# A permutation matrix in 16 bits, widened on another engine, and a new order of tasks

## The chip, the cores and the metric

One core of a Trainium2 chip. The metric is the device time of one execution in microseconds (us), the median of several runs.

## What is computed

32 graphs of 256 nodes: `x` is 32 x 256 x 64, `adj` 32 x 256 x 256 and sparse (about 1.5% of the pairs, and the diagonal). For each graph:

```python
mask = (adj > 0.0)
xj_proj = x @ W1[:F]
diff = x[:, :, None, :] - x[:, None, :, :]
h = relu(xj_proj[:, :, None, :] + diff @ W1[F:] + b1)      # H = 192
hm = einsum('bjkh,bjk->bjh', h, mask)
out = layernorm(x + hm @ W2 + sum(mask, -1)[..., None] * b2)
```

So each node j adds up relu(u_j - v_k) over its neighbours k, with u = x (W1a + W1b) + b1 and v = x W1b.

## The kernel before, in words

**Tiling.** Two graphs make a pair, 16 pairs in all. A pair has TILES = 4 tiles of P = 128 nodes. The 192 hidden columns are split into a "main" part (128, one group per tile) and a "tail" part (64, the two graphs packed together).

**A pair's path.** VectorE makes the 0/1 mask from the adjacency tiles (`masks`, L1583), counts neighbours (`count_masks`, `count_least`, `count_rest`) and compares the counts with levels (`sort_key`). TensorE adds that up (`keys`), and VectorE turns it into a rank for each node (`ranks`) and into a permutation matrix that sorts nodes by their number of neighbours (`permutation`, L1650): 1 where the place equals the rank. TensorE transposes and permutes the masks with it (`turn_masks`), ScalarE copies them out of PSUM (`copy_maskT`), TensorE numbers each node's neighbours (`number_slots`), ScalarE copies that (`copy_slots`), and VectorE makes one-hot matrices, one for each "slot", the j-th neighbour of every node (`select`, pieces 0 to 10). TensorE sorts x (`sort_x`, with the permutation in f32, `excess_tail` beside it), forms u (`hidden_u_main`, `hidden_u_tail`) and v (`hidden_v`); ScalarE copies u, and v in two forms (`high_v` f16, `full_v` f32), and GpSimd (POOL) takes the difference (`low_v`, L661). ScalarE writes u into PSUM banks (`seed`), TensorE adds the gathered neighbours' -v (`gather`, L1327), and VectorE adds relu of the result into `sums` (`add`, L1796; the last units are shared, `add_joint`, L1810). At the end come `project`, `copy_y`, `unsort_y` (with the transposed permutation from `turn_perm` and `copy_permT`), `add_residual`, `statistics`, and on POOL `moments`, `centre` and `scale`.

**The permutation's type.** `perm` is f32, because `sort_x` multiplies f32 by it. The matmuls in 16 bits read it through `perm16()`, the upper half of each f32 word:

```python
def perm16(side, c):
    return perm[side][:, c, :].bitcast(BF16).rearrange("p (r two) -> p r two", two=2)[:, :, 1]
```

**Scales.** Because v is split into f16 parts, the weights are scaled by a power of two. For pair 0 that comes from the maximum of its x (`first_max`) and of the weights (`prepare_weights`, L1675, on VectorE; `add_weights_up`, L1120, on TensorE; `weight_top`, L1680, and `first_scales`, L1695 to L1712, on VectorE), for all others from all of x: ScalarE sums it in four chunks (`sum_chunk`, L815), VectorE takes the most (`most`), TensorE spreads it (`spread_x`, L1132), and VectorE makes the scales (`scales`). `hidden_u_main(Pair(0, 0))` and `hidden_u_tail(Pair(0, 0))` wait for `scales_ready[0]`. `keep_busy` (L1375) and `set_banks` (L1143) are matmuls on ones.

**What sets the order.** Every engine has its own list of tasks, in program order, with semaphores between them. Each list has a head that is written out (pairs 0 and 1), a `body(pair)` run for pairs 1 to 13 (of these, 4 to 9 in a hardware loop of two pairs a turn), and a written-out tail (pairs 14 and 15). In one body, different engines work on up to five different pairs. A task waits at its place in the list, and with it all that stands behind it on that engine. The buffers of most tiles are double, by the pair's parity. SyncE issues all DMAs through one queue, in its own list: first `adj` 0, constants, x 0, weights, xT 0, `adj` 1, all of x in four chunks, x 1, xT 1, `adj` 2, `adj` 3, then x 2, which waits for `xb_ready` (from `residual(Pair(0, 0))` on POOL) and `xs_ready`.

In the head VectorE runs, in this order: `masks` to `sort_key` of pair 0, `ranks`, `permutation`, `ranks_above`, `prepare_weights`, `masks(Pair(0, 1))`, `count_masks(Pair(0, 1))`, `count_given(Pair(0, 0))`, `count_least(Pair(0, 1))`, `first_max`, `weight_top`, `first_scales`, `masks(Pair(0, 2))`, then selections of pair 0, `most` and `scales`.

Should a graph have more neighbours than the slots hold, a general path runs behind all this (`general_loop`); with these inputs it doesn't.

## Time and profile before

| what | value |
|---|---|
| runs, device time | 252.63, 252.81, 254.0 us; median 252.81 |
| profiled execution | 252.74 us, span 250.9 us |
| busy | PE 235.9 (94%), VectorE 226.6 (90%), ScalarE 209.8 (84%), POOL 121.4 (48%) |
| DMA | 18.20 MB, the 16 engines at 21.7% of the span |

The span runs from the first to the last instruction that the profile shows, and the device time has some 2 us around it. Names: PE is TensorE's matmul, PEld its weight load, DVE VectorE, ACT ScalarE, POOL GpSimd, SP SyncE. L1327 is a line of the kernel. Matmuls are pipelined and their spans overlap. An instruction on VectorE or ScalarE starts some 0.1 us before the one ahead of it ends, so the time from start to start is a little shorter than the duration.

### The profile page before, as it was taken

What the parts mean: (1) busy time and instruction counts of PE and PEld (TensorE: products, weight loads), DVE (VectorE), ACT (ScalarE), POOL (GpSimd) and SP (SyncE); (2) the same over time, 40 slices, a digit from 0 to 9 for tenths busy, and PEclk for the clock granted to TensorE, in tenths of its full rate; (3) what the DMA queues carried; (4) which work ended last, traced back from release to release, by engine and by line L of the source; (5) the groups of instructions that cost most, each with busy time, mean ns of one, the idle gap of its engine ahead of it and who ended that gap; (6) DMA issues with size and microseconds to landing.
All of it is one profiled execution on the core that took longest, in us unless ns stands there. A gap on an engine that the chain in (4) does not pass through costs nothing. (4 is left out here: it accounts for less than half of the span.)

```text
span 250.9 us, 9244 instructions
## 1 busy us (share of the span) xinstructions
PE 235.9 (94%) x2810; PEld 188.7 (75%) x2813; DVE 226.6 (90%) x778; ACT 209.8 (84%) x572; POOL 121.4 (48%) x288
## 2 busy tenths in 40 slices
PE   7947989999999999999999999999999999998992
PEld 2524758888787878787888878887878888886761
DVE  4757699999999999999999999999999999997763
ACT  2384888989998989899899999898999989987631
POOL 1124444363645637463736364563736483576225
PEclk9985899999999999999999999999999999999998
DMA  6983003221212213131313021221310110000002
GB/s 201 357 325 106 3 4 123 70 84 30 70 54 78 73 55 96 44 107 42 106 39 107 14 74 59 64 82 47 105 44 25 43 46 0 25 24 1 3 8 63
DMA packets 10550, 18.20 MB, mean 73 GB/s; under 512 B 1296, under 2 KB 7696, under 8 KB 10512
## 3 DMA queue, kind: packets, MB, share of 16 engines
q1 hardware_dynamic: 10512, 17.73, 21.7%
q8 instruction: 19, 0.31, 0.5%
q14 instruction: 19, 0.16, 0.2%
HBM read 15.63 MB, written 2.10 MB: 71 GB/s over the span
## 5 line engine op out<-in xcount | busy, mean ns | idle before, releaser
L1327 PE MATMUL ring<-hot,vh 128*128 128x128 bf16 (+9 forms) x768 | 117.4, 255 | 1.3 <-ACT ring L914 1.0
L1327 PE MATMUL ring<-hot,vl 128*128 128x128 bf16 (+9 forms) x768 | 116.3, 251 | 0.0
L1796 DVE SCALAR_TENSOR_TENSOR sums<-ring,sums 128x256 f32<-128x256 f32 (+10 forms) x240 | 97.8, 428 | 4.3 <-PE ring L1327 1.9
L1327 PEld LDWEIGHTS ring<-hot,vh 128*128 128x128 f16 (+1 forms) x768 | 62.0, 104 | 23.6 <-issue 16.8
L1327 PEld LDWEIGHTS ring<-hot,vl 128*128 128x128 f16 (+1 forms) x768 | 61.9, 103 | 2.4
L661 POOL TENSOR_TENSOR vl<-vf,vh 128x384 f16<-128x384 f32 x32 | 29.7, 929 | 63.2 <-ACT vf L870 59.4
L903 ACT COPY ring<-u_sb 128x192 f32<-128x192 f32 (+8 forms) x160 | 49.3, 359 | 7.4 <-DVE sums L1796 7.4
L900 ACT COPY ring<-u_sb 128x512 f32<-128x512 f32 (+1 forms) x80 | 43.3, 559 | 0.4 <-issue 0.2
L715 POOL TENSOR_TENSOR sums<-taken,sums 128x512 f32<-128x512 f32 x16 | 20.7, 1292 | 27.1 <-ACT taken L932 27.1
L821 ACT CAST maskT<-bx 128x512 bf16<-128x512 f32 x32 | 18.5, 586 | 14.3 <-PE bx L1171 13.8
L1771 DVE TENSOR_SCALAR hot<-slotT 128x944 bf16<-128x944 f16 (+6 forms) x112 | 28.6, 280 | 0.0
L1591 DVE TENSOR_REDUCE counts<-mask 128x8 f32<-128x1024 bf16 x16 | 19.4, 1214 | 0.1
L828 ACT CAST slotT<-bx 128x512 f16<-128x512 f32 x32 | 18.9, 592 | 0.0
L1290 PEld LDWEIGHTS bx<-w2ms,sums 128*128 128x128 f32 x128 | 17.9, 192 | 1.3 <-DVE sums L1824 0.6
L1304 PE MATMUL bx<-y_sb,permT 128*128 128x64 f32 x128 | 18.6, 272 | 0.0
L1290 PE MATMUL bx<-w2ms,sums 128*128 128x64 f32 x128 | 17.9, 263 | 0.4 <-DVE sums L1824 0.4
L863 ACT CAST vh<-bx 128x384 f16<-128x384 f32 x32 | 15.4, 482 | 3.2 <-PE bx L1257 3.2
L1304 PEld LDWEIGHTS bx<-y_sb,permT 128*128 128x128 f32 x128 | 16.6, 191 | 0.9 <-ACT y_sb L884 0.5
L1188 PE MATMUL bx<-maskT,cst_half 128*128 128x128 bf16 x128 | 16.1, 221 | 0.1
L1583 DVE TENSOR_SCALAR mask<-adj_sb 128x1024 bf16<-128x1024 f32 x16 | 11.0, 688 | 5.4 <-DMA adj_sb<-adj 5.4
L1257 PE MATMUL bx<-w1vs,xT_sb 64*128 64x192 f32 x128 | 15.5, 362 | 0.3 <-ACT u_sb L855 0.3
L870 ACT COPY vf<-bx 128x384 f32<-128x384 f32 x32 | 15.5, 489 | 0.0
(119 smaller groups left out, 463.7 us busy)
## 6 DMA issues: line engine op xcount, KB each, us to landing
adj_sb<-adj SPq DMA_DIRECT2D x16, 512.0 KB, 3.7
x_sb<-x_pairs SPq DMA_DIRECT2D x16, 128.0 KB, 2.3
xT_sb<-xT SPq DMA_DIRECT2D x16, 128.0 KB, 2.1
x_all<-x SPq DMA_DIRECT2D x4, 512.0 KB, 7.9
out<-o_sb SPq DMA_DIRECT2D x16, 128.0 KB, 1.7
wts<-weights SPq DMA_DIRECT2D x1, 417.0 KB, 4.8
cst_general<-general SPq DMA_DIRECT2D x1, 256.0 KB, 3.2
cst_half<-half SPq DMA_DIRECT2D x1, 137.0 KB, 3.1
```

The lines of the kernel that those rows point to most:

```text
L661: eng.tensor_tensor(vl[pair.side][:, c, :], vf[:, c, :], vh[pair.side][:, c, :], ALU.subtract).then_inc(vl_ready, 1)
L715: eng.tensor_tensor(to, taken[piece][:, :, :], to, ALU.add).then_inc(taken_added, 1)
L821: eng.copy(maskT[:, g * NT:g * NT + NT, :].rearrange("p t r -> p (t r)"), (bx1, bx2)[g][:, :]).then_inc(maskT_copied, 1)
L828: eng.copy(slotT[:, g * NT:g * NT + NT, :].rearrange("p t r -> p (t r)"), (bx0, bx1)[g][:, :]).then_inc(slots_copied, 1)
L900: last = eng.copy(to, u.unsqueeze(1).broadcast_to([P, sum(map(whole, pieces)), n, P]))
L903: last = eng.copy(view(pair, part, unit, piece), u[:, :, 0:PIECES[piece][2]])
L1290: eng.matmul(to[:, g * O:g * O + O], sums[pair.side][:, NT + g * NT + t, :], w2ms[scaled(pair)][:, :], start=(g == 0), stop=False, skip_gr ...
L1304: last = eng.matmul(bx3[:, (TILES + c) * O:(TILES + c + 1) * O], permT[pair.side][:, c, :], y_sb[:, t * 2 + g, :], start=True, stop=True)
L1327: return eng.matmul(to if part == "main" else to[g * HT:g * HT + HT], values, selection, start=False, stop=final, skip_group_check=True)
L1591: eng.tensor_reduce(counts[pair.side][:, :, :].rearrange("p g c -> p (g c)"), mask[pair.side][:, :, :].rearrange("p c (k n) -> p (c k) n", ...
L1771: eng.tensor_scalar(to[:, :, :, off:off + n], slots, float(MARK + s), None, ALU.is_equal).then_inc(hot_ready, 1)
L1796: eng.scalar_tensor_tensor(out=to, in0=view(pair, part, unit, piece), scalar=0.0, in1=to, op0=ALU.max, op1=ALU.add).then_inc(added[part], 1)
```

## The change

`permutation` writes a bf16 tile `perm16` (`rank` becomes f16), and a new ScalarE task copies it to the f32 tile `perm`, for `sort_x` alone. The bf16 matmuls read `perm16` densely. The lists of all engines but SyncE are put in another order, most of all in head and tail.

```diff
-        rank = sb("rank", [P, TILES])
-        perm = both("perm", [P, TILES, P])
+        rank = sb("rank", [P, TILES], F16)
+        perm16, perm = both("perm16", [P, TILES, P], BF16), both("perm", [P, TILES, P])
...
+            def widen_perm(pair):
+                eng.wait_ge(perm_ready, pair.n + 1)
+                if pair.follows(2):
+                    eng.wait_ge(xs_ready, pair.n - 1)
+                eng.copy(perm[pair.side][:, :, :].rearrange("p c r -> p (c r)"),
+                         perm16[pair.side][:, :, :].rearrange("p c r -> p (c r)")).then_inc(perm_widened, 1)
...
-                                          perm16(pair.side, g * NT + t), start=True, stop=True)
+                                          perm16[pair.side][:, g * NT + t, :], start=True, stop=True)
...
             def sort_x(pair):
-                eng.wait_ge(perm_ready, pair.n + 1)
+                eng.wait_ge(perm_widened, pair.n + 1)
...
-                eng.tensor_tensor(perm[pair.side][:, :, :], places.unsqueeze(1).broadcast_to([P, TILES, P]),
+                eng.tensor_tensor(perm16[pair.side][:, :, :], places.unsqueeze(1).broadcast_to([P, TILES, P]),
                                   rank[:, :].unsqueeze(2).broadcast_to([P, TILES, P]), ALU.is_equal).then_inc(perm_ready, 1)
```

The loop bodies. ScalarE: `widen_perm(new)` ahead of `copy_maskT(new, 0)`, and `copy_permT` goes from the end of the body to the start of the next. VectorE: `add(older, "tail", 7)` goes behind `select(old, 9)`. POOL: `scale(older)` goes between `low_v(new, 0)` and `low_v(new, 1)`. TensorE: `gather(new, "main", 6)` is no longer cut in two across the loop's edge.

VectorE's head:

```diff
             sort_key(Pair(0, 0))
+            first_max()
             ranks(Pair(0, 0))
             permutation(Pair(0, 0))
             ranks_above(Pair(0, 0))
+            count_given(Pair(0, 0))
+            masks(Pair(0, 1))
+            masks(Pair(0, 2))
             prepare_weights()
-            masks(Pair(0, 1))
-            count_masks(Pair(0, 1))
-            count_given(Pair(0, 0))
-            count_least(Pair(0, 1))
-            first_max()
             weight_top()
             first_scales()
-            masks(Pair(0, 2))
+            make_ident()
+            count_masks(Pair(0, 1))
             select(Pair(0, 0), 0)
             select(Pair(0, 0), 1)
             select(Pair(0, 0), 2)
-            most()
             select(Pair(0, 0), 3)
             select(Pair(0, 0), 4)
+            count_least(Pair(0, 1))
+            most()
+            select(Pair(0, 0), 5)
+            count_rest(Pair(0, 1))
             scales()
-            count_rest(Pair(0, 1))
-            select(Pair(0, 0), 5)
             scale_down(0)
-            make_ident()
             run(eng, body)
```

TensorE's head:

```diff
             turn_masks(Pair(0, 0), 1)
+            add_first_up()
+            number_slots(Pair(0, 0), 0)
+            number_slots(Pair(0, 0), 1)
             add_weights_up()
-            number_slots(Pair(0, 0), 0)
             sort_x(Pair(0, 0))
+            excess_tail(Pair(0, 0))
             keep_busy(1)
-            number_slots(Pair(0, 0), 1)
-            excess_tail(Pair(0, 0))
-            add_first_up()
             keep_busy(3)
+            hidden_u_tail(Pair(0, 0))
+            hidden_u_main(Pair(0, 0))
             set_banks(0)
-            excess_main(Pair(0, 0))
-            hidden_u_main(Pair(0, 0))
-            hidden_u_tail(Pair(0, 0))
             spread_x()
             hidden_v(Pair(0, 0))
+            keys(Pair(0, 1))
+            excess_main(Pair(0, 0))
             set_banks(1)
-            keys(Pair(0, 1))
...
```

ScalarE's head becomes: `widen_perm(0)`, the two `copy_maskT`, `sum_chunk(0)`, `copy_slots(0)`, `sum_chunk(1)`, `copy_xs`, `copy_slots(1)`, `sum_chunk(2)`, `copy_u_tail`, `sum_chunk(3)`, `copy_u_main`, `full_v(0)`, `high_v(0)`, a seed, `high_v(1)`, `full_v(1)`, `widen_perm(1)`, all for pair 0 but the last. POOL's head becomes: `degrees`, `corrections`, `add_weights`, `degrees(1)`, `low_v(0, 0)`, `corrections(1)`, `low_v(0, 1)`, `scale_inputs`, `add_taken(0)`, `low_v(1, 0)`, `degree_bias(0)`, `degrees(2)`, `scale_outputs(1)`, `residual(0)`, `scale_outputs(0)`, `low_v(1, 1)`, `corrections(2)`, `degree_bias(1)`.

In the tail the lists of pairs 14 and 15 are interleaved anew. At its end TensorE runs `unsort_y(14)`, `project(15)`, `unsort_y(15)`, `keep_busy_last(2)`, `add_over` (before: `add_over` ahead of `project(15)`, `keep_busy_last(2)` ahead of `unsort_y(15)`), and ScalarE's `sum_over` stands behind `deviation(14)`; POOL's `scale(14)` waits for that sum in both.

## Rows read from the trace of the kernel before

**Rows 1.** Busy time by stretch (stretch, its length, each engine, granted clock, DMA share).

```profile
7.00:17.23 10.23, 8.03 (x62) 4.34 (x61) 6.04 (x18) 6.98 (x15) 2.33 (x5) 1.00 1.00 380
17.23:27.47 10.24, 6.96 (x45) 4.71 (x47) 8.21 (x30) 5.42 (x13) 4.94 (x11) 0.50 0.24 82
...
40.53:206.00 165.47, 165.31 (x2122) 138.00 (x2117) 163.50 (x565) 153.92 (x426) 86.20 (x204) 1.00 0.22 68
...
123.43:137.24 13.81, 13.81 (x185) 11.66 (x183) 13.74 (x48) 12.84 (x36) 6.84 (x16) 1.00 0.28 94
```

**Rows 2.** What VectorE waited for, 40.53 to 205 (total us, times, longest).

```profile
DVE sums L1796 <- PE ring L1327: 0.3, 1, 0.3
```

**Rows 3.** Groups by line and form (busy us, mean ns), VectorE.

```profile
L1650 DVE TENSOR_TENSOR perm<-cst_half,rank 128x512 f32<-128x512 f16 x16 | 11.0, 686 | 0.0
...
L1776 DVE TENSOR_TENSOR hot<-slotT,cst_half 128x288 bf16<-128x288 f16 x16 | 7.4, 464 | 0.0
...
L1762 DVE TENSOR_TENSOR hot<-slotT,cst_half 128x512 bf16<-128x512 f16 x16 | 6.7, 420 | 0.0
...
L1627 DVE TENSOR_TENSOR reaches<-rest,cst_order 128x72 bf16<-128x72 bf16 x16 | 3.6, 228 | 0.1
```

**Rows 4.** The same view, ScalarE.

```profile
L900 ACT COPY ring<-u_sb 128x512 f32<-128x512 f32 x64 | 37.2, 603 | 0.2 <-issue 0.2
...
L815 ACT ACTIVATE x_abs<-x_all 128x1024 f32<-128x1024 f32 x4 | 4.2, 1062 | 0.9 <-DMA x_all<-x 0.9
```

**Rows 5.** SyncE's issue of `adj_sb` 2 and 3; issues 8.4 to 10; x loads.

```profile
8.54 2.15 SPq L514 DMA_DIRECT2D adj_sb<-adj  x2
...
adj_sb<-adj SPq DMA_DIRECT2D x1, 512.0 KB, 8.6
...
x_sb<-x_pairs SPq DMA_DIRECT2D x16, 128.0 KB, 2.3
```

**Rows 6.** Order of time (start us, us), VectorE, 0 to 42.

```profile
8.83 0.34 DVE L1675 SCALAR_TENSOR_TENSOR w_abs<-wts 64x192 f32<-64x192 f32 x1
...
12.04 0.35 DVE L1680 TENSOR_REDUCE w_top<-ring 128x1 f32<-128x192 f32 x1
12.77 0.22 DVE L1695 TENSOR_SCALAR bound<-ring,w_top 128x1 f32<-128x1 f32 x1 [0.39 <-PE ring L1125]
...
13.53 0.88 DVE L1711 TENSOR_SCALAR w1abs<-w1ab,up_bits 128x256 f32<-128x256 f32 x1
...
17.20 0.69 DVE L1583 TENSOR_SCALAR mask<-adj_sb 128x1024 bf16<-128x1024 f32 x1 [2.55 <-DMA adj_sb<-adj]
...
22.52 0.22 DVE L1636 TENSOR_TENSOR steps_ahead<-bx,reaches 128x64 f32<-128x64 f32 x1 [0.88 <-PE bx L1155]
...
29.53 0.50 DVE L1759 TENSOR_SCALAR hot<-slotT 128x512 bf16<-128x512 f16 x2 [1.62 <-ACT slotT L828]
```

**Rows 7.** The same view, TensorE.

```profile
9.39 0.59 PE L1120 MATMUL ring<-w_abs,ones 64*128 64x192 f32 x2
...
10.55 0.66 PE L1201 MATMUL bx<-perm,x_sb 128*64 128x128 f32 x8
...
14.47 0.70 PE L1236 MATMUL bx<-xs,w1abs 64*128 64x256 f32 x4 [0.41 <-DVE w1abs L1711]
...
18.75 0.80 PE L1132 MATMUL ring<-ident,x_most 128*128 128x128 f32 x2 [2.15 <-DVE x_most L1685]
19.48 1.65 PE L1257 MATMUL bx<-w1vs,xT_sb 64*128 64x192 f32 x8
21.06 1.03 PE L1143 MATMUL ring<-ones 128*128 128x512 bf16 x2
...
40.53 0.61 PE L1201 MATMUL bx<-perm,x_sb 128*64 128x128 f32 x8
```

**Rows 8.** What ScalarE waited for, 40.53 to 206.

```profile
ACT maskT L821 <- PE bx L1171: 4.9, 17, 0.8
```

**Rows 9.** What VectorE waited for, 40.53 to 250.9.

```profile
DVE sums L1810 <- ACT small L939: 2.2, 3, 1.6
```

More of the change, by code:

```diff
@@ L740, in body @@
                     low_v(new, 0)
[L741 removed]
                 if has(-2):
                     scale(older)
+                if has(1):
+                    low_v(new, 1)
                 if has(2):
@@ L959, in body @@
                 elder, older, old, new = pair.at(-3), pair.at(-2), pair.at(-1), pair.at(1)
+                if has(-1):
+                    copy_permT(old)
                 if has(0):
@@ L1002, in body @@
                     seed_joint(old)
-                if has(0):
-                    copy_permT(pair)
             eng.wait_ge(consts_loaded["single"], 16)
+            widen_perm(Pair(0, 0))
             copy_maskT(Pair(0, 0), 0)
@@ L1642, in ranks @@
                         eng.wait_ge(above_ready, pair.n)
-                eng.tensor_reduce(rank[:, :], steps_ahead[:, :, :], AX.X, ALU.add).then_inc(ranks_ready, 1)
+                with nc.allow_low_precision(reason="whole numbers of at most 128"):
+                    eng.tensor_reduce(rank[:, :], steps_ahead[:, :, :], AX.X, ALU.add).then_inc(ranks_ready, 1)
             def permutation(pair):
@@ L1899, in body @@
                     select(old, 9)
+                if has(-2):
+                    add(older, "tail", 7)
                 if has(0):
```

222 lines of the change are left out of this document (110 added, 112 removed).

## The prediction

> **What bounds the kernel now.** I read four views in this order: the busy time by stretch, what VectorE waited for, the groups by line and form, and the order of time of the head. In one period of the middle (the loop works one pair in 13.81 us) VectorE is busy for 13.74 us, and over 40.53 to 206.00 for 163.50 of 165.47 us [rows 1]. In that whole stretch its waits come to 0.3 us [rows 2]. TensorE shows 100% busy too, but its matmul spans overlap, so that share alone proves nothing; that VectorE never waits does. So VectorE sets the middle: only VectorE time that is removed shortens a pair, and a task that is only moved there changes nothing while its inputs are in time. ScalarE is busy for 12.84 us of the period and has 0.97 us free [rows 1]. The head, up to about 29.5 us, is another matter: there each engine waits, and what counts is the chain that ends in the first selections of pair 1. Whatever the head is late, the middle is late by, since nothing in the middle is idle to catch up.
>
> The time: the span is 250.9 us and the profiled execution took 252.74, 1.8 us more around the span; the median of the runs is 252.81. I add to the median.
>
> **The permutation in 16 bits.** It is 128x512 on VectorE, one per pair, at 686 ns [rows 3]. Its result becomes bf16, `rank` becomes f16 and `places` is f16 already. What decides is how fast such an instruction runs when one input is a single value repeated along the innermost dimension (`rank` broadcast over 128). Three rows with 16-bit tensors on both sides bear on it [rows 3]. L1762, 512 elements, both inputs with neighbouring elements, takes 420 ns. L1776 is 288 elements, its `slotT` operand repeated along the innermost dimension, and takes 464 ns: more than the 512 of L1762. L1627, 72 elements with `rest` repeated in the same way, takes 228 ns. From L1627 to L1776 there are 216 elements and 236 ns, 1.09 ns each; carried on to 512 that gives 464 + 224 x 1.09 = 708 ns, and the full-width row is 686. The new instruction is built like L1776 and L1627, so I take 686 ns still: **0 us saved**. The other end is L1762's 420 ns, 0.266 us for each of 16 pairs, 4.3 us. The two small instructions on `rank` have 64 elements and can save nothing that counts.
>
> The Trainium skill weighs on both sides here. "VectorE: DVE Perf Modes", perf-mode tier table, gives `tensor_tensor` on bf16 in SBUF twice the rate: the sum would then be 4.3 us lower, the first rival. "Vector Engine (DVE) Microarchitecture Reference", section 5.1, wants a step of plus or minus 1 on every operand and reports one element read again and again in a two-source operation at the 1x rate; by that rule nothing is saved, and L1776 agrees with its 464 ns.
>
> **The widening** is new on ScalarE: 128x512 bf16 to f32, SBUF to SBUF, 16 times. The nearest row is L900, 512 elements from SBUF at 603 ns; the far end is L815, 1024 elements at 1062 ns [rows 4]. I take 0.6 us, some 0.52 from start to start. A period's ScalarE work goes from 12.84 to 13.4 us, under 13.81. Its place is just ahead of the two mask copies, where ScalarE waits for TensorE anyway: 4.9 us in 17 waits over the middle, about 0.3 at each [rows 8]. The two waits of a pair hide the 0.52 us; the first mask copy ends about 0.3 us later, and the slot numbering behind it on TensorE comes half a microsecond after that copy. So I cost it at **0 in the middle**. If that cover were gone it would be 0.5 us a pair. `sort_x` now waits for the widening, but comes a whole pair later. TensorE's reading of every second 16-bit word goes; I give it 0, since VectorE is the bound.
>
> **The moves in the loop.** On VectorE the tail addition of piece 7 goes behind two selections; all inputs are early, 0. On POOL `scale` goes between the two `low_v`, on ScalarE `copy_permT` merely crosses the loop's edge, on TensorE the last gather is no longer cut: 0, none of these engines is the bound.
>
> **The head: this is where the time goes.** VectorE runs its list in order, and `masks(Pair(0, 2))` now stands ahead of `prepare_weights`, `weight_top` and `first_scales`. Its adjacency tiles are issued at 8.54 us and land 8.6 us later, 17.2 us, in a stretch in which the DMA engines are 100% busy [rows 1, 5]; SyncE's list is not touched, so that landing stays. Before, the third mask waited for it too, for 2.55 us, but with the scales of pair 0 already done; `w_abs` ran at 8.83 and `w1abs` ended at 13.53 + 0.88 = 14.41 [rows 6].
> Step by step, at the half TensorE clock of 17.23 to 27.47 (0.50 granted, that is 1.2 GHz; it fell after a stretch with TensorE partly idle, and the new order leaves it idler, so I keep the fall) [rows 1]:
> - masks 17.20 to 17.81, `w_abs` 0.34: 18.15.
> - `add_weights_up` on TensorE, 0.59 us at full clock, about 0.9 at half: 19.2. TensorE stands at it from about 11.5 us, and behind it wait `sort_x(0)`, so the copy of xs on ScalarE, and behind that two of the four sums over x.
> - `w_top` 0.35, then from `bound` to the end of `w1abs` as before, 14.41 - 12.77 = 1.64: 21.2.
> - TensorE meanwhile: `sort_x`, 0.66 at full clock, some 0.9 here; the excess, its four small matmuls, some 0.3; four busy matmuls at about half of the 1.03 that the two of `set_banks` took at this clock, less their overlap: 21.8. Then `hidden_u_tail` and `hidden_u_main`, 0.70 at full clock for the second, about 1.0 each here: 23.8. `set_banks(0)`, 1.03 with its overlap: 24.7. VectorE has `most()` done by 24.5, after the counts, five selections and the fourth sum over x.
> - `spread_x` 0.8, and `hidden_v(0)` 1.65 at this clock: it starts at 25.5 and ends at 27.1. Before it started at 19.48 [rows 7]: **6.0 us late**.
> - From there the old chain: v copied, keys, ranks of pair 1 at about 28.3 instead of 22.52, 5.8 late. The first selection of pair 1 had 1.6 us of waiting before it at 29.53 [rows 6], of which the new order keeps about 0.7: **4.9 us late** at 34.4. There the period begins, and the lag stays.
> Ends: 4.0 us, if TensorE is back at full clock early and the selections wait less; 6.0 if nothing is recovered.
> Also moved on POOL: `residual(Pair(0, 0))` now stands behind `low_v` of pair 1, at some 36 us, and SyncE's load of x for pair 2 waits for it with four loads queued behind. Done at about 42.5, with the 4.9 in it, and 2.3 us to land [rows 5], it is there by 45; pair 2 was sorted at 40.53 [rows 7], 45.4 with the 4.9. So 0, but the cover is thin: each tenth more on POOL would hold TensorE by a tenth, once.
>
> **The tail.** VectorE waits there for ScalarE's clamps, 2.2 us in three waits, and for little else [rows 9]. A new order can recover at most those and about 1.5 us of others; nothing excludes a loss, for `sum_over` now ends only after the last `unsort_y`, with `scale(14)` behind it on POOL. I take -0.8, ends -2.6 and +0.7.
>
> **Sum:** 0 + 0 + 4.9 - 0.8 = +4.1; 252.8 + 4.1 = 256.9, which I put as **256.8 us**, 1.6% slower. Its own range is 254.5 to 258.9.
>
> **Rivals.**
> 1. The permutation runs at L1762's rate, 420 ns. Then VectorE, the bound, loses 16 x 0.266 = 4.3 us and pays for the head: 256.8 - 4.3 = 252.5, no change that can be measured (I count 0.5% as that, 1.3 us). It decides from about 0.2 us saved a pair. For: all its tensors have 16 bits. Against: L1776 and L1627. 0.14; a third of it with a better tail is faster.
> 2. The masks' wait is off the path: the tiles of pair 2 land early, or the scales are not the last thing `hidden_v` needs. The head is then the old one, the tail gives 0.8 to 1.3: 251.5, faster. It decides from a landing before about 12 us. Against: DMA at 100% and an untouched SyncE list. 0.06.
> 3. ScalarE becomes the bound. If the widening costs nearer L815's 1062 ns, the second mask copy is 0.4 us later in each pair, and its few waits for VectorE's additions no longer fit: about 0.3 us x 14 = 4.2 us, 261.0. For: 13.4 of 13.81 us. Against: the waits it falls into. 0.08.
> 4. TensorE's clock stays at 1.2 GHz for one more stretch, since it idles from 11.5 to 18.2. The first gathers would run at half rate: about 4 us more, 260.8. Against: from 17.2 to 27.5 it does about as much as before, after which the clock came back [rows 1]. 0.10.
>
> **How the numbers follow.** Forecast 0.62; rivals 0.14, 0.06, 0.08, 0.10. Slower: 0.62 + 0.08 + 0.10 = 0.80. Same: most of rival 1, 0.10. Faster: rival 2 and the rest of rival 1, 0.10. The range takes in rival 1's 252.5 and the nearer half of rivals 3 and 4: 252.3 to 260.5. Both signs do not share the weight, so it is the forecast's range widened.
>
> **What would show it.** In the new profile: the third mask on VectorE still at 17.2, with an idle time of nearly 7 us before it; `w1abs` of pair 0 ending at about 21 instead of 14.4; `hidden_v(0)` at about 25.5; the permutation at 686 ns; a period of 13.81 us; ScalarE 13.4 us busy in it. The forecast falls if the permutation row shows 420 ns, if the period is not 13.8 us, or if `hidden_v(0)` starts before 22 us.

## The result and the profile after

| | kernel before | changed kernel |
|---|---|---|
| median of the runs | 253.03 us (252.63 to 254.0, 4 runs) | 261.17 us (260.89 to 261.94, 4 runs) |
| profiled execution, span | 252.74, 250.9 us | 261.94, 260.1 us |
| VectorE, ScalarE busy | 226.6, 209.8 us | 227.7, 216.9 us |

The ratio of the times is 1.0321 [1.0283, 1.0358]: 3.2% slower, 8.1 us, where 256.8 was forecast (252.3 to 260.5). The same kernel run again beside other runs of the kernel before (15) gave 260.31 us against 252.98, 1.0269 [1.0232, 1.0306]; so the loss is 7 to 8 us. One of those six runs, 262.86 us, is in the slow state, and all ratios are of fast runs alone. The two profiled executions differ by 9.2 us, and that is the sum which the rows below divide.

The busy time by stretch, to set beside [rows 1] (the first two stretches end where the granted clock changes in this kernel):

```profile
7.00:12.30 5.30, 3.32 (x31) 2.01 (x31) 2.82 (x7) 2.28 (x4) 1.03 (x3) 1.00 0.99 340
12.30:22.50 10.20, 4.01 (x19) 2.46 (x20) 3.71 (x12) 3.68 (x9) 0.00 (x0) 0.50 0.52 203
40.53:206.00 165.47, 163.52 (x2078) 135.52 (x2077) 162.96 (x561) 158.01 (x435) 88.03 (x204) 1.00 0.23 71
123.43:137.24 13.81, 13.78 (x177) 11.44 (x175) 13.74 (x48) 13.29 (x38) 7.30 (x18) 1.00 0.21 65
```

A window of 13.81 us in the middle has VectorE busy for 13.74 us, as before; ScalarE went from 12.84 to 13.29. The period itself is 13.6 us in both kernels: the 11 pairs from pair 2's first sums to pair 13's take 149.63 us before and 149.68 after. The loss is not in the middle. The groups by line, ScalarE's widening and mask copy, then the permutation on VectorE:

```profile
L818 ACT CAST perm<-perm 128x512 f32<-128x512 bf16 x16 | 10.0, 623 | 7.1 <-DVE perm L1658 7.1
L825 ACT CAST maskT<-bx 128x512 bf16<-128x512 f32 x32 | 18.1, 589 | 1.3 <-PE bx L1180 1.1
```
```profile
L1658 DVE TENSOR_TENSOR perm<-cst_half,rank 128x512 bf16<-128x512 f16 x16 | 10.9, 682 | 0.0
```

The permutation still takes 682 ns (686 in f32, [rows 3]). From 40.53 to 206 the mask copy waits for TensorE for 0.3 us, where it was 4.9 [rows 8]: the widening has eaten those waits. Without it, under the same new orders (2), they are 5.1 us.

VectorE in order of time (start us, us), beside [rows 6]:

```profile
17.48 0.69 DVE L1590 TENSOR_SCALAR mask<-adj_sb 128x1024 bf16<-128x1024 f32 x1 [6.78 <-DMA adj_sb<-adj]
18.09 0.34 DVE L1683 SCALAR_TENSOR_TENSOR w_abs<-wts 64x192 f32<-64x192 f32 x1
19.53 0.36 DVE L1688 TENSOR_REDUCE w_top<-ring 128x1 f32<-128x192 f32 x1 [1.09 <-PE ring L1129]
...
20.76 0.35 DVE L1719 TENSOR_SCALAR w1abs<-w1ab,up_bits 128x256 f32<-128x256 f32 x1
...
27.81 0.23 DVE L1643 TENSOR_TENSOR steps_ahead<-bx,reaches 128x64 f32<-128x64 f32 x1 [0.71 <-PE bx L1164]
...
34.05 0.49 DVE L1767 TENSOR_SCALAR hot<-slotT 128x512 bf16<-128x512 f16 x2 [0.64 <-ACT slotT L832]
```

And TensorE, beside [rows 7]:

```profile
18.49 1.00 PE L1129 MATMUL ring<-w_abs,ones 64*128 64x192 f32 x2 [7.58 <-DVE w_abs L1683]
...
25.64 0.92 PE L1266 MATMUL bx<-w1vs,xT_sb 64*128 64x192 f32 x8 [0.25 <-ACT u_sb L849]
...
46.10 0.66 PE L1210 MATMUL bx<-perm,x_sb 128*64 128x128 f32 x8 [0.89 <-DMA x_sb<-x_pairs]
```

This is the chain that was forecast: VectorE waits 6.78 us at the third mask with the weights behind it, TensorE then 7.58 us for `w_abs`, and `hidden_v(0)` starts at 25.64 instead of 19.48. The last of these rows is the loss that was not forecast there: the sort of pair 2's x waits for its load.

The tail, all engines in order of time:

```profile
251.18 1.94 PE L1313 MATMUL bx<-y_sb,permT 128*128 128x64 f32 x8 [0.46 <-ACT y_sb L888]
...
253.90 0.37 PE L1371 MATMUL bx<-over,ones 128*1 128x64 f32 x2
...
254.31 0.21 ACT L959 ACTIVATE over_junk<-bx 1x64 f32<-1x64 f32 x1 [2.99 <-PE bx L1371]
...
254.68 0.46 POOL L720 CAST over_int<-over_sum 1x1 int32<-1x1 f32 x1 [2.51 <-ACT over_junk L959]
255.10 0.60 POOL L675 TENSOR_TENSOR o_sb<-centred,rstd 128x256 f32<-128x256 f32 x1
...
255.81 0.18 DVE L1856 RECIPROCAL rstd<-std 128x4 f32<-128x4 f32 x1 [0.71 <-POOL o_sb L675]
```

The last `rstd` is held by POOL's `scale(14)`, that by the sum of `over`, and that by `add_over`, which TensorE runs behind the last `unsort_y` and two scratch matmuls.

The 9.2 us, each as the difference of the same instruction's start in the two traces, and beside it the same steps in the profiled execution of 15, the same kernel once more (rounded, so the columns can be 0.1 off their sums). "First sums" is `start_sums`, L1750 here and L1742 before.

| step, us later than in the kernel before | changed | changed again (15) |
|---|---|---|
| head, to the first sums of pair 1 (41.25 against 36.72; the first selection, 34.05 against 29.53, says the same) | 4.5 | 5.6 |
| load of x for pair 2, to the first sums of pair 13 (206.03 against 200.29) | 1.2 | 1.1 |
| interleaving, to `z` of pair 14 (248.54 against 242.30) | 0.5 | 0.5 |
| last `unsort_y`, 1.94 us at the half clock, to `z` of pair 15 (253.16 against 246.08) | 0.8 | 0.0 |
| the sum's chain, to VectorE's last instruction (256.08 against 248.20) | 0.8 | 0.1 |
| behind it, mostly the last store | 1.3 | 1.2 |
| span | 9.2 | 8.5 |

### The profile page after: what moved, and what is told of

Read it like the earlier page. It is cut to its first block, busy times and chain, and to the rows that moved or that the text cites. A ratio compares the mean times of both kernels' runs of the same rounds, so it can differ in the third digit from the quotient of the medians.

```text
span 260.1 us, 9280 instructions
## 1 busy us (share of the span) xinstructions
PE 235.8 (91%) x2813; PEld 187.6 (72%) x2813; DVE 227.7 (88%) x778; ACT 216.9 (83%) x588; POOL 122.7 (47%) x288
## 4 chain that ended last, share of the span: by engine, by line
PE 64%; DVE 8%; issue 8%; POOL 5%; ACT 5%; DMA 5%; SPq 3%; DVEq 0%; POOLq 0%; ACTq 0%
PE ring L1336 31%; PE bx L1266 4%; PE bx L1313 4%; PE bx L1299 4%; DMA adj_sb<-adj 3%; PE bx L1245 3%; PE bx L1302 3%; PE bx L1210 3%; PE bx L1253 2%; PE bx L1180 2%; DVE sums L1804 2%; PE bx L1197 2%; DVE sums L1750 2%; PE bx L1234 1%; DMA x_sb<-x_pairs 1%
## 5 line engine op out<-in xcount | busy, mean ns | idle before, releaser
L907 ACT COPY ring<-u_sb 128x192 f32<-128x192 f32 (+8 forms) x160 | 49.9, 359 | 7.2 <-DVE sums L1804 6.8
L1313 PE MATMUL bx<-y_sb,permT 128*128 128x64 f32 x128 | 19.4, 281 | 0.5 <-ACT y_sb L888 0.5
L1313 PEld LDWEIGHTS bx<-y_sb,permT 128*128 128x128 f32 x128 | 17.4, 200 | 1.0 <-ACT y_sb L888 0.7
L611 POOL TENSOR_TENSOR excess<-deg,given 128x4 bf16<-128x4 f32 x16 | 4.1, 256 | 25.5 <-DVE given L1675 25.5
L818 ACT CAST perm<-perm 128x512 f32<-128x512 bf16 x16 | 10.0, 623 | 7.1 <-DVE perm L1658 7.1
```

Source lines behind the costliest of these rows:

```text
L907: last = eng.copy(view(pair, part, unit, piece), u[:, :, 0:PIECES[piece][2]])
L1313: last = eng.matmul(bx3[:, (TILES + c) * O:(TILES + c + 1) * O], permT[pair.side][:, c, :], y_sb[:, t * 2 + g, :], start=True, stop=True)
```

## The experiments

The first four are about the types, the next six about the head, the rest about the tail. Ratios are to the kernel before, run on the same chip; its medians lay between 252.91 and 253.08.

### 1. The types alone

The kernel before with the new tiles and the widening (and the wait of `sort_x` for it), all orders old.

```diff
+                    widen_perm(new)
                     copy_maskT(new, 0)
```

> The kernel before with the types alone: bf16 perm16 by VectorE, widened by ScalarE ahead of the two mask copies, every list in its old order. Theory (VectorE sets the middle and takes 686 ns either way; the widening falls into ScalarE's waits): 253.0 us, within 0.5, period 13.6 us on average. Rival A (16 bits help, 420 ns): 249. Rival B (ScalarE becomes the bound): over 255.

Measured: 253.51 us, 1.0021 [1.0001, 1.0041]. The groups by line, and the middle window:

```profile
L1659 DVE TENSOR_TENSOR perm<-cst_half,rank 128x512 bf16<-128x512 f16 x16 | 11.0, 686 | 0.0
```
```profile
123.43:137.24 13.81, 13.81 (x187) 11.64 (x184) 13.74 (x48) 13.22 (x37) 6.87 (x16) 1.00 0.26 86
```

The 16 bits save nothing and the widening costs nothing per pair; 0.2% is all that both do to the kernel.

### 2. The orders alone

The changed kernel with the permutation in f32 and no widening.

```diff
-                    widen_perm(new)
                     copy_maskT(new, 0)
```

> The changed kernel with all new orders, but the permutation in f32 as before and no widening on ScalarE. Theory (VectorE takes 686 ns for it either way and ScalarE's 0.6 us falls into its waits): same period of 13.6 us on average, median 261.2 within 0.4. Rival A (the widening costs in the middle): 0.1 us or more a pair, 259.6 or less. Rival B (reading every second 16-bit word slows TensorE): slower than 261.6.

Measured: 262.34 us, 1.0366 [1.0339, 1.0394]. From pair 4's first sums to pair 13's, 84.42 to 206.76, it is 122.34 us; with the widening 83.73 to 206.03, 122.30. Taking the widening off ScalarE gives nothing back: rival 3 falls. With 1, the whole loss is in the orders. The time is 1 to 2 us above the changed kernel's, past the 261.6 us from which the expectation counted for its rival B. But the matmuls of `turn_masks`, which read the permutation, take 219 ns with every second word (L1172 here) and 219 ns densely (L1180), so that rival isn't borne out; where the extra microsecond comes from is open.

### 3. VectorE's prices by themselves

Seven scratch instructions in the wait for the third mask of the changed kernel. `every` is the places repeated over the 4 tiles, `again` the rank repeated along the row, `other` a plain row repeated over the tiles.

```diff
+            eng.tensor_tensor(m16[0][:, :, :], every, other, ALU.is_equal)
+            eng.tensor_tensor(m32[0][:, :, :], every, other, ALU.is_equal)
+            eng.tensor_tensor(m16[1][:, :, :], every, again, ALU.is_equal)
+            eng.tensor_tensor(m16[2][:, :, :], again, every, ALU.is_equal)
+            eng.tensor_tensor(m32[1][:, :, :], every, again, ALU.is_equal)
+            eng.tensor_scalar(m16[3][:, 0, :], places, rank[:, 0:1], None, ALU.is_equal)
+            eng.tensor_scalar(m16[4][:, 0, :], places, 3.0, None, ALU.is_equal)
```

> The changed kernel with seven extra instructions on VectorE that write scratch tiles nobody reads, in the 6.8 us in which VectorE waits for the tiles of the third mask. It measures VectorE's prices by themselves: the places repeated over the three tiles compared with a tile's rank repeated along the row (384 elements), written in 16 bits, with the operands swapped, and written in 32 bits; the same with a plain 128-element row as second operand, written in 16 and in 32 bits; and one 128-element comparison with a scalar read from a tile and one with a constant. Theory that the repeated rank (an operand whose innermost step is zero) is what keeps the permutation at 686 ns: the three forms with the rank repeated take 650 to 700 ns whatever the output and the order, the 16-bit form without it takes 400 to 480 ns. Rival, that the 16-bit output never helps where the operands are repeated over the tiles: the form without the rank takes about 680 ns too. For the scalar form the run of four scalars gave 270 ns; if the scalar from a tile is the reason, the constant takes about 190 ns. All seven together are some 3.5 us and lie in the wait, so the time stays at 260 to 262 us.

Measured: 261.77 us. The groups by form, VectorE, 8 to 20 us (the lines L1974 to L1980 are the seven, in that order):

```profile
L1975 DVE TENSOR_TENSOR m<-cst_half 128x512 f32<-128x512 f16 x1 | 0.7, 679 | 0.0
L1977 DVE TENSOR_TENSOR m<-rank,cst_half 128x512 bf16<-128x512 f16 x1 | 0.7, 679 | 0.0
L1976 DVE TENSOR_TENSOR m<-cst_half,rank 128x512 bf16<-128x512 f16 x1 | 0.7, 678 | 0.0
L1978 DVE TENSOR_TENSOR m<-cst_half,rank 128x512 f32<-128x512 f16 x1 | 0.7, 677 | 0.0
L1974 DVE TENSOR_TENSOR m<-cst_half 128x512 bf16<-128x512 f16 x1 | 0.4, 410 | 0.0
...
L1979 DVE TENSOR_SCALAR m<-cst_half,rank 128x128 bf16<-128x128 f16 x1 | 0.2, 242 | 0.0
...
L1980 DVE TENSOR_SCALAR m<-cst_half 128x128 bf16<-128x128 f16 x1 | 0.2, 180 | 0.0
```

Both conditions are needed: a 16-bit result and no operand repeated along the innermost dimension give 410 ns; either one missing gives 677 to 679, and the order of the operands changes nothing. (The operands have 4 x 128 = 512 elements; the expectation's 384 was a slip, its times were for these instructions.) Repeating over the tiles does no harm.

### 4. Four scalars in place of the repeated rank

The types of 1, and the permutation as four instructions that read the rank as a scalar per partition.

```diff
+                for c in range(TILES):
+                    last = eng.tensor_scalar(perm16[pair.side][:, c, :], places, rank[:, c:c + 1], None, ALU.is_equal)
```

> As the kernel with the types alone, but the permutation is made by four TENSOR_SCALAR instructions of 128 elements, each with one column of rank (f32) as its per-partition scalar, so that no operand repeats one element. Theory: each takes about 190 ns, 0.10 to 0.15 us from start to start as the 128-element selection does, 0.4 to 0.55 us in all against 0.61 for the one of 686 ns; VectorE as the bound passes that on: 0.05 to 0.2 us a pair, 250 to 252.3 us. Rival (reading the scalar costs as much as is saved, or VectorE is not the bound): 252.8 to 253.5.

Measured: 255.45 us, 1.0098 [1.0069, 1.0128], above the expected range and above the rival's too. The group, and two of its pairs in order of time:

```profile
L1660 DVE TENSOR_SCALAR perm<-cst_half,rank 128x128 bf16<-128x128 f16 x64 | 13.1, 270 | 0.0
```
```profile
36.84 0.74 DVE L1660 TENSOR_SCALAR perm<-cst_half,rank 128x128 bf16<-128x128 f16 x4
...
50.83 1.40 DVE L1660 TENSOR_SCALAR perm<-cst_half,rank 128x128 bf16<-128x128 f16 x4
```

The mean of 270 ns hides two sorts. 62 of the 64 take 242 to 255 ns and start 0.16 us apart, so that four of them hold VectorE for 0.65 us up to the start of the next instruction, where the one instruction held it for 0.60. In two pairs, at 23.15 and 50.83 us, one of the four takes 0.91 us, both times while a `low_v` of POOL is running. Pair 13's first sums are 2.07 us late: 1.4 from these two, the rest from 0.05 us in each other pair. A scalar read from a tile costs 242 to 255 ns where a constant costs 180 (3), so this way round the repeated rank is no saving.

### 5. The third mask behind the head

The changed kernel, one task moved.

```diff
             masks(Pair(0, 1))
-            masks(Pair(0, 2))
             prepare_weights()
...
             scale_down(0)
+            masks(Pair(0, 2))
             run(eng, body)
```

> The changed kernel with one line moved: the third mask of VectorE's head goes from ahead of prepare_weights to behind scale_down(0). Theory (the wait for the adjacency tiles of pair 2 holds the whole head, 4.5 us): w_abs at about 10.7 us instead of 18.1, hidden_v(0) at 18 to 19 instead of 25.64, the median falls by 4 to 5.5 us from 261.2, to 255.7 to 257.2. Rival (the head is late for other reasons, the new lists of TensorE and ScalarE): hidden_v(0) stays behind 23 us and the median above 259.

Measured: 253.17 us, 1.0025 [0.9981, 1.0069]: 7 to 8 us back from one line, more than expected. VectorE and TensorE in order of time:

```profile
10.74 0.34 DVE L1683 SCALAR_TENSOR_TENSOR w_abs<-wts 64x192 f32<-64x192 f32 x1
...
19.33 0.68 DVE L1590 TENSOR_SCALAR mask<-adj_sb 128x1024 bf16<-128x1024 f32 x1
```
```profile
18.40 0.92 PE L1266 MATMUL bx<-w1vs,xT_sb 64*128 64x192 f32 x8 [0.25 <-ACT u_sb L849]
```

`hidden_v(0)` starts 7.2 us earlier than in the changed kernel and 1.1 earlier than in the kernel before. The wait for pair 2's x is gone here, with `residual(0)` at its new place. In another profiled execution of the same kernel (span 253.6 us instead of 251.4) `hidden_v(0)` starts at 18.42 and pair 13's first sums at 199.46, 6.6 us earlier than in the changed kernel, but there the wait is back:

```profile
39.61 0.66 PE L1210 MATMUL bx<-perm,x_sb 128*64 128x128 f32 x8 [0.41 <-DMA x_sb<-x_pairs]
```

So the late head is not the only thing that decides on that wait (see 10). Pair 13's first sums are also 0.8 us ahead of the kernel before, and that is no gain of the other moves: with the old orders and the third mask last (8) they come at 198.73, earlier still. The expectation had priced the mask's wait in the changed kernel and left out what this mask costs at its old place, 1.5 us (8).

### 6. The third mask back where it was

The changed kernel with the mask behind `first_scales`.

```diff
-            masks(Pair(0, 2))
             prepare_weights()
             weight_top()
             first_scales()
+            masks(Pair(0, 2))
             make_ident()
```

> The changed kernel with the third mask moved only behind first_scales, the place that it had relative to weight_top and first_scales in the kernel before; the rest as changed. Theory, that what costs is VectorE waiting for the tiles with the weights queued behind it: w_abs starts at about 10.5 us, hidden_v(0) at 18.5 to 20 instead of 25.64, and the time is 253.2 to 255, 1 at most above the version with the mask behind scale_down(0). Rival, that at this place the mask still waits (its tiles landed at about 17.2, first_scales ends at about 13 here because ident is made behind it): VectorE waits some 3 to 4 us with the selections of pair 0 behind it, hidden_v(0) is at 19 to 21, start_sums of pair 1 at 38 to 39.5, and the time is 255 to 257.5.

Measured: 257.7 us, 1.0203 [1.0161, 1.0245]; the rival's case, a little past its upper end. VectorE:

```profile
13.22 0.35 DVE L1719 TENSOR_SCALAR w1abs<-w1ab,up_bits 128x256 f32<-128x256 f32 x1
...
17.12 0.69 DVE L1590 TENSOR_SCALAR mask<-adj_sb 128x1024 bf16<-128x1024 f32 x1 [3.32 <-DMA adj_sb<-adj]
```

The scales are early, but the tasks which the change has moved behind this point (`count_least`, `most` and the selections) now wait 3.32 us, and `hidden_v(0)` starts at 20.98. What counts is which work stands behind the wait: with all of it behind, 261; with half, 257.7; with none, 253.2.

### 7. The masks' move alone, on the kernel before

```diff
+            masks(Pair(0, 1))
+            masks(Pair(0, 2))
             prepare_weights()
-            masks(Pair(0, 1))
             count_masks(Pair(0, 1))
...
             first_scales()
-            masks(Pair(0, 2))
```

> One part of the change alone on the kernel before: masks(1) and masks(2) moved ahead of prepare_weights, permutation, tail and the other orders left as they were. Theory, that this move is the head's whole loss: VectorE waits for the tiles of the third pair until about 17.2 us as in the changed kernel, hidden_v(0) starts at about 25.6 instead of 19.48, start_sums of pair 0 and 1 come 4.5 to 5.5 us later, and the time is 257 to 260, 1.6 to 2.8 per cent over. Rival, that the other reorderings of the head (the orders of the ranks and of the weights' part on TensorE and ScalarE) carry half of it: 254.5 to 256.

Measured: 260.4 us, 1.0269 [1.0229, 1.0309]. The mask is at 17.29 behind 6.58 us of waiting, and TensorE:

```profile
27.75 0.92 PE L1257 MATMUL bx<-w1vs,xT_sb 64*128 64x192 f32 x8 [1.33 <-ACT u_sb L845]
```

That one move alone costs 7.3 us, a little more than the expected range. Pair 13's first sums are 8.6 us late (208.84), more than the 5.7 of the full change: TensorE's list here keeps the slot numbering behind `add_weights_up`, so more stands in the wait, and the granted clock is at 0.5 for one more stretch (30.8 to 37.6).

### 8. The mask last, on the kernel before

```diff
             first_scales()
-            masks(Pair(0, 2))
...
             make_ident()
+            masks(Pair(0, 2))
             run(eng, body)
```

> The kernel before with its third mask moved from behind residual(0) to behind make_ident, so that VectorE's w_abs, w_top and w1abs and TensorE's w_bound come without it. Theory, that the mask ahead of the weights delays the head in either kernel: here VectorE does not wait for its tiles, so only the mask's own time ahead of w_abs goes and hidden_v(0) starts at 17.9 to 19.5 instead of 19.48; the time is 251 to 252.5, 0.2 to 0.8 per cent under the kernel before. Rival, that the head of the kernel before is set by the ranks and by the clock: no difference, 252.5 to 253.5.

Measured: 251.59 us, 0.9945 [0.9923, 0.9967], the only version under both kernels. The mask runs at 19.26 without any wait and `hidden_v(0)` starts at 18.30. The 2.55 us that the kernel before waits at its third mask [rows 6] were worth 1.5 us.

### 9. The clock during the wait

The changed kernel, TensorE's idle wait filled.

```diff
             number_slots(Pair(0, 0), 1)
+            keep_busy(28)
             add_weights_up()
```

> The changed kernel with 28 more scratch matmuls on TensorE in the 7.6 us that it idles ahead of add_weights_up; nothing else moves. It separates the wait from the clock: if part of what the third mask cost at the head is TensorE's granted clock falling in or behind its idle wait (0.5 from 12.3 to 22.5 us in the changed kernel, 17.2 to 27.5 in the kernel before), the stretches at 0.5 move and the time falls by 1 to 3 us, to 258 to 260. Theory that the wait alone costs: the stretches may move, but start_sums of pair 0 and 1 stay within 0.3 us and the time stays at 260 to 261.5. Rival on the other side: the scratch matmuls bring the half clock over hidden_v and the ranks, and the time rises by 1 to 4 us, to 261.5 to 265.

Measured: 260.28 us, 1.0272 [1.0243, 1.0301]. The busy time by stretch, to be read against the stretches above:

```profile
12.30:22.50 10.20, 9.08 (x50) 3.98 (x47) 4.31 (x14) 4.64 (x11) 0.45 (x1) 1.00 0.51 200
...
27.70:31.20 3.50, 2.98 (x30) 2.60 (x29) 2.44 (x6) 2.96 (x7) 2.41 (x6) 0.51 0.01 2
```

With the wait filled the granted clock stays at 1.00 (2.4 GHz) from 12.3 to 22.5 us, where it was 0.50 (1.2 GHz) with TensorE busy for 4.01 of 10.20 us. `hidden_v(0)` comes at 23.92 instead of 25.64, pair 1's first sums at 40.34 instead of 41.25, and the profiled execution took 259.39. Another 1.0 us of its gain is not the clock: the load of x for pair 2 landed 2.0 us after its issue and TensorE did not wait for it. The median does not follow: 260.28 against 261.17 and 260.31 for the changed kernel on other chips. The half clock is part of the head's loss in the traces, but what it is worth in the median, between nothing and 1 us, stays open.

### 10. The residual early

The changed kernel.

```diff
             add_weights()
+            degree_bias(Pair(0, 0))
+            residual(Pair(0, 0))
             degrees(Pair(0, 1))
...
             low_v(Pair(0, 1), 0)
-            degree_bias(Pair(0, 0))
             degrees(Pair(0, 2))
             scale_outputs(1)
-            residual(Pair(0, 0))
```

> The changed kernel with degree_bias(0) and residual(0) on POOL put back behind add_weights, so that the load of x for pair 2 is issued at once. Theory (the 0.89 us that TensorE waits for this load at 45 us is passed on in full by the middle, where nothing is idle): that wait goes, the start of sums of pair 2 stands 1.0 to 1.2 us earlier, median 260.0. Rival (VectorE catches it up, as it has waits around it): same median, 261.2.

Measured: 260.99 us, 1.0305 [1.0275, 1.0335]. The sort of pair 2's x starts with no wait, and pair 2's first sums come 14.0 us after pair 1's instead of 15.1. The wait is gone as expected, but the time is nearer to the rival's 261.2 than to the theory's 260.0 and cannot be told from the changed kernel's. In a profiled execution the half clock lasts from 12.1 to 25.7 us and puts pair 1's first sums at 42.43 instead of 41.25. Besides, the wait isn't always there to be saved: with `residual(0)` at its new place, the load landed 3.4, 3.3 and 3.4 us after its issue in the profiled executions of the changed kernel, of 15 and of 2, and 2.0 us after it in those of 3, 9 and 11, where pair 2's first sums come 14.1 us after pair 1's as well. The 1.2 us is shown in some of the traces, not in the medians.

### 11. The sum early

The changed kernel, with `sum_beyond` behind `add_taken(Pair(0, 15), 0)` on POOL as well.

```diff
             unsort_y(Pair(0, 14))
+            add_over()
             project(Pair(0, 15))
             unsort_y(Pair(0, 15))
             keep_busy_last(2)
-            add_over()
...
             clamp_small(Pair(0, 15))
+            sum_over()
             copy_y(Pair(0, 15))
             deviation(Pair(0, 14))
-            sum_over()
```

> The changed kernel with the sum over what is left beyond the slots taken early again: sum_beyond behind add_taken(15) on POOL, add_over ahead of project(15) on TensorE, sum_over ahead of copy_y(15) on ScalarE. Theory (all engines' branch waits for this sum; scale(14) on POOL stands behind it, and TensorE's branch, 3.7 us long, is exposed when it starts only at 256.0): rstd of pair 15 0.7 us earlier after z, TensorE's branch ends before the last store has landed, median lower by 1.5 to 2.1 us, 259.1 to 259.7. Rival (the last store is the end anyway): at most 0.7 us lower, 260.5.

Measured: 259.3 us, 1.0241 [1.0214, 1.0269]. The last `rstd` comes 1.52 us after the one before it instead of 2.31 and no longer waits for POOL. In 15, where the last `unsort_y` of the changed kernel ran at full clock, the distance was 1.62 us with the sum still late: 0.1 us of the 0.8 is the order, the rest comes with the half clock. Behind VectorE's last instruction the span goes on for 3.4 us instead of 4.1 (3.9 in 15). Against the changed kernel's 260.31 and 261.17 the median is 1 to 2 us lower, as expected.

### 12. The sum late, on the kernel before

The same tasks moved the other way; TensorE's part is shown, and on ScalarE `sum_over` goes behind `deviation(14)`, on POOL `keep_sum` behind `centre(14)`.

```diff
             unsort_y(Pair(0, 14))
-            add_over()
             project(Pair(0, 15))
-            keep_busy_last(2)
             unsort_y(Pair(0, 15))
+            keep_busy_last(2)
+            add_over()
```

> The kernel before with the order of the sum's parts alone taken from the changed kernel: add_over behind the last unsort_y and the scratch matmuls on TensorE, sum_over behind the last copy_y and deviation(14) on ScalarE, keep_sum behind centre(14) on POOL. Theory, that the late sum holds the last pair's scale and then the kernel's end through TensorE's branch: the last rstd comes about 2.3 us behind the one before it instead of 1.5, the branch of 3.6 us begins behind the last store instead of 2.4 us ahead of it, and the time rises by 1.3 to 2.2 us, to 254.3 to 255.3 (ratio 1.005 to 1.009). Rival, that the sum is late only because the interleaving before it is: no difference, 252.6 to 253.6.

Measured: 253.92 us, 1.0049 [1.0029, 1.0070], just short of the expected rise. Only 0.15 us of it is at the last `rstd` (248.09 against 247.94); the rest is behind it. The trace's records of branches, which the views by engine leave out, have one on TensorE, for the sum. Its start and duration, against the time from the end of the last write of `o_sb` to the store's completion, in seven of the profiled executions:

| kernel | branch starts, before that write ends | branch takes | the store takes |
|---|---|---|---|
| before | 2.84 us | 3.61 us | 1.74 us |
| third mask last on before (8) | 2.84 | 3.80 | 1.76 |
| three moves (13) | 1.97 | 3.57 | 2.05 |
| sum early (11) | 1.59 | 2.90 | 2.44 |
| sum late on before (12) | 0.40 | 2.92 | 2.54 |
| changed | 0.46 | 3.73 | 2.91 |
| changed, wait filled (9) | 0.37 | 0.36 | 2.99 |

In the other ten profiled executions the store takes 1.7 to 2.4 us where the branch starts 2.8 us ahead, and 2.8 to 3.4 us where it starts 0.4 to 0.6 us ahead. So a late sum goes with a long store, but within either group the store varies by up to 0.9 us. The 1.2 us between the lines of the two kernels are nearly all that is lost behind VectorE's last instruction in that pair of executions; the median of this run, 1.0 us up with nothing else moved, shows that most of it is the sum's place. It is not the branch's length: in the last line it takes 0.36 us and the store is as long. What lengthens the store when the sum is late stays open.

### 13. The three moves together

The changed kernel with 5, 10 and 11.

> The changed kernel with the three moves together: third mask behind scale_down(0), residual(0) early, the last sum early. If the three account for what was lost: the head 1 us ahead of the kernel before, no wait for x of pair 2, TensorE's last branch hidden; 250.5 to 252 us. Rival (they overlap, or one of them has no effect): 253 or more.

Measured: 252.73 us, 0.9992 [0.9967, 1.0017]. Three moves return the whole loss, and no more than that, where a gain was expected: pair 13's first sums are 1.1 us earlier than in the kernel before, and the tail loses these 1.1 us again.

### 14. The old tail under the new head

The head of 13, the loop bodies and the tail lists of the kernel before, the types kept.

> The changed kernel's head with two of the three moves (third mask last, residual early), under the middle and the tail of the kernel before, with the 16-bit permutation and its widening kept. Theory, that the new interleaving of the last pairs costs 1 us (start_sums of pair 13 to 14 took 14.54 us with the three moves and 13.57 in the kernel before): pair 13 to the end of the span takes 50.6 us instead of 51.7, and the time is 251.2 to 252.2, 0.3 to 0.7 per cent under the kernel before. Rival, that the tail's extra microsecond belongs to the phase in which it is entered: 252.5 to 253.2, as with the three moves.

Measured: 253.98 us, 1.0050 [1.0026, 1.0073]. What VectorE waited for in the tail, first with the new interleaving (13), then with the old one (14):

```profile
DVE sums L1804 <- POOL sums L711: 1.6, 1, 1.6
DVE sums L1818 <- PE ring L1336: 1.1, 2, 0.9
DVE sums L1818 <- ACT small L943: 0.8, 2, 0.4
```
```profile
DVE sums L1819 <- ACT small L942: 1.9, 3, 1.2
DVE sums L1805 <- PE ring L1335: 0.9, 2, 0.7
DVE sums L1805 <- POOL sums L711: 0.4, 1, 0.4
```

From pair 13's first sums to pair 14's it is 13.59 us instead of 14.54, and to the end of the span 50.4 instead of 51.7, as the theory said: the new order cuts the waits for the clamps [rows 9] from 2.2 to 0.8 and gets a wait for POOL's sums of 1.6 in return. The waits are not the whole account. Between the first sums of pairs 13 and 14, two selections of the new order (13) are slow:

```profile
206.75 0.83 DVE L1770 TENSOR_TENSOR hot<-slotT,cst_half 128x512 bf16<-128x512 f16 x1
...
208.67 0.57 DVE L1779 TENSOR_SCALAR hot<-slotT 128x768 bf16<-128x768 f16 x1
```

The same forms take 0.42 and 0.36 us elsewhere, so this is 0.6 of the 0.95 us. A third, at 221.23, takes 1.43 us instead of 0.36. Each of the three starts while an instruction of POOL is running and ends behind it; the changed kernel has the same three. The old tail has two such selections, 0.73 and 0.51 us for 0.30 and 0.21. Why these are slow and others beside POOL are not is not shown.

But the time did not fall. In this combination pair 1's first sums come at 36.86 instead of 35.52, with a stretch at half clock from 24.8 to 28.3; why the head comes later here is not shown. So the term is shown, but not as a gain of a whole kernel.

### 15. The changed kernel again

> The changed kernel itself once more, for a second sample of its time on the chip of the runs beside it. 261.2 us, 260.5 to 262. If its runs fall into two groups about 1 us apart, the granted clock differs from run to run; the kernel without the widening (262.3) would then not be slower than it.

Measured: 260.31 us (258.86 to 262.86). Its profile has a second half-clock stretch at 30.0 to 33.4, pair 1's first sums at 42.32 instead of 41.25, and the last `unsort_y` at full clock (1.10 us instead of 1.94). The last `rstd` then comes 1.62 us after the one before it, with the sum as late as ever. So 1 us at the head and 1.5 at the tail, the slow `unsort_y` and most of the sum's chain, come and go with the execution. The wait for pair 2's x is there in both, 0.78 us here.

## Why the prediction missed

**The middle was right.** The permutation kept its price, 682 ns, by the rows that it was likened to, and 3 shows why. By the tier table of "VectorE: DVE Perf Modes" in the Trainium skill it would have run at twice the rate; the trace does not agree, with 682 ns. By section 5.1 of "Vector Engine (DVE) Microarchitecture Reference" in the Trainium skill it keeps the full price; the trace agrees, with 678 ns where one operand is repeated and 410 ns where none is (3). The widening hid in ScalarE's waits for the masks as costed (1 and 2), at 623 ns for 0.6. Rivals 1 and 3 are out. The prediction read 13.81 us as the period; that is the length of its window, and the period is 13.6 us in both kernels. Nothing in the sum hangs on it.

**The head was right in cause and close in size.** Third mask forecast at 17.20, measured 17.48; `hidden_v(0)` 25.5, measured 25.64; first selection of pair 1 34.4, measured 34.05. In 15 the head costs 5.6 us, still inside the ends of 4.0 to 6.0. Two single terms were too long. `w1abs` took 0.35 us, not the 0.88 of [rows 6]. In the kernel before it ran beside an instruction of `residual(Pair(0, 0))` on POOL, which the change has moved away:

```profile
13.54 0.73 POOL L650 TENSOR_TENSOR xb<-db,x_sb 128x256 f32<-128x256 f32 x1
```

It takes 0.88 us in the five profiled executions with this neighbour and 0.35 in the twelve without. But it is off the path here: `hidden_u_tail` started at 22.37 without waiting for it. The other term: the full clock came back at 22.5, so `hidden_v` took 0.92 instead of 1.65, and the ranks of pair 1 came at 27.81, not 28.3. Rival 2 is out: the wait is the path (5, 7). Rival 4 happens, at a quarter of its price: the extra stretch at half clock costs about 1 us (15), not 4. That the measured 260.3 to 261.2 us lies at the prices of rivals 3 and 4, 261.0 and 260.8, is chance: neither mechanism carries the loss.

**Failed: "So 0, but the cover is thin", the load of x for pair 2.** The supply was taken as 42.5 plus 2.3 us, the demand as 45.4. SyncE's issues in the changed kernel:

```profile
42.70 0.33 SPq L523 DMA_DIRECT2D x_sb<-x_pairs  x1
43.07 0.43 SPq L515 DMA_DIRECT2D xT_sb<-xT  x1
43.55 1.46 SPq L510 DMA_DIRECT2D adj_sb<-adj  x1
```

The load was issued when forecast and the sort was due at 45.2, but the tile was there only at 46.1: 3.4 us after its issue, not the 2.3 of the median load [rows 5]. The time from issue to landing of this one load, in the changed kernel and in 9:

```profile
x_sb<-x_pairs SPq DMA_DIRECT2D x1, 128.0 KB, 3.4
```
```profile
x_sb<-x_pairs SPq DMA_DIRECT2D x1, 128.0 KB, 2.0
```

The failed term is the landing time, a median put in where the cover was 0.4 us; the wait is 0.89 us and the whole step 1.2. It is 3.3 or 3.4 us in three profiled executions and 2.0 in three others with the same issues at the same distances (10). So the two loads issued on its heels, one of them 512 KB, don't explain it; in the kernel before two follow as closely, and the load landed after 1.9 us. What makes the difference stays open.

**Failed: "I take -0.8" for the tail**, measured at +3.5 of the 9.2 in the profiled execution and +1.8 of the 8.5 in 15, both outside its ends of -2.6 to +0.7. It priced the tail by the waits that a new order could win back, and named the late sum without following it. Following it gives `add_over`, `sum_over`, POOL's conversion, `scale(14)`, the last `rstd`: 0.1 us at full clock (15; 0.15 in 12), and 0.8 where the scratch matmuls and `add_over` run at the half clock. The interleaving trades waits and has slower selections: 0.5 (14). The slower last `unsort_y`, 0.8 or nothing, and the longer store, 1.2 to 1.3, have no row in the trace of before; the first differs by execution (15), the second goes with the late sum (12).

So +4.1 should read 4.5 + 1.2 + 3.5 = 9.2 in the one profiled execution and 5.6 + 1.1 + 1.8 = 8.5 in the other; the medians have 8.1 and 7.3. Even the upper ends of the prediction's own terms, 6.0 and 0.7, added to 252.8 reach only 259.5. Putting the mask last returns more than the head's 4.5, because it also takes away what that mask costs at its old place, 1.5 us (8), and in some executions the load's wait (5).

## What to carry over

When a task that waits for a load is moved up an in-order list, price all that is now behind it, on every engine, and run the loads' landing times against it, with their spread and not their median: here one line was worth 7 to 8 us, and moving the same line the other way on the old kernel gave the only gain (251.59 us). Before narrowing a type for speed, look for an operand repeated along the innermost dimension. In a written-out tail follow every side product up to the last store; the waits that a new order can win back say nothing of those that it makes.

## What the runs showed that was not expected

- A VectorE scalar operand read from a tile costs 242 to 255 ns for 128 elements, a constant 180; started one behind the other such instructions come 0.16 us apart (3, 4).
- VectorE instructions that take over 0.15 us more than the median of their form are few, 92 in the seventeen profiled executions, and every one of them began while an instruction of POOL was running, such as the selection of 1.43 us for 0.36 at 221.23 in 13. More than 400 an execution overlap POOL and all but these 3 to 7 keep their price; what sets them apart is not shown (4, 14).
- The branch on a loaded value at the kernel's end takes TensorE 2.9 to 4.1 us in sixteen of seventeen executions and 0.36 us in one; the last store takes 1.7 to 2.4 us with an early sum and 2.5 to 3.4 with a late one, whatever the branch takes (12).
- One and the same load, issued at the same distances from its neighbours, lands after 2.0 us in three executions and after 3.3 or 3.4 in three others (10).
- TensorE's granted clock was 0.50 over 12.3 to 22.5 us with 4.01 us of work in it, and 1.00 with the same wait filled by scratch matmuls; a half-clock stretch then came at 27.7 (9). Where the stretches fall differs between executions of one kernel (15).
